# Attention scores of two image pairs in one TensorE pass, on other PSUM banks, with the transposes and tables around them recut

## The reference, cut to what matters

```python
h = tok(x)                                   # 16 x 64 x 64
tokens = concatenate([q, k, v]) = the same 64 rows three times
h = concatenate([cls_tok, h], axis=1)        # 16 x 193 x 64, class token first
attn = softmax(q k^T / 8) + rel_bias         # 8 heads of 8 features, 193 x 193
h = h + layernorm(attn @ v)                  # attention block
w = layernorm(h) @ wr + br                   # feed-forward block: router weight,
sel = top 95 of 193 tokens by w              # the largest ones take part
h = h + (mlp(sel) * w_sel scattered back) + layernorm(h)
```

## Time and profile before

| | |
|---|---|
| median of 3 runs | 88.4 us (88.22 to 92.36) |
| the profiled execution | 88.42 us, of it 86.5 us in the span |
| outside the span | 1.92 us |
| granted TensorE clock, mean | 0.985 |
| TensorE busy | 78.2 us (90%) |
| VectorE busy | 57.5 us (66%) |
| ScalarE busy | 55.8 us (65%) |
| GpSimd busy | 18.2 us (21%) |

### The profile page before, as it was taken

The page is one execution under the profiler, slowest core; times in us unless marked ns, Lnnn a source line. Parts: engine busy times, 40 slices in busy tenths (PEclk is TensorE's granted clock), DMA queues, the critical chain, the costliest instruction groups (busy, mean ns, idle before and its releaser), DMA issues.

```text
span 86.5 us, 1796 instructions
## 1 busy us (share of the span) xinstructions
PE 78.2 (90%) x638; PEld 49.8 (58%) x638; DVE 57.5 (66%) x188; ACT 55.8 (65%) x122; POOL 18.2 (21%) x31
## 2 busy tenths in 40 slices
PE   3999999999799999999998998999999799999800
PEld 1585758698478457769787865654523242446500
DVE  0299339439465994979989338389925799993860
ACT  0518247788558389885927272799999968995000
POOL 7000000000024553569150000000086300000620
PEclk9999999999999999999999999999999999999995
DMA  1937991000000000000000000000000000000045
GB/s 28 284 139 240 322 361 39 0 0 4 8 0 0 0 11 0 0 0 0 0 8 0 0 0 8 0 0 0 0 0 0 4 0 0 0 0 8 0 152 213
DMA packets 2568, 3.95 MB, mean 46 GB/s; under 512 B 544, under 2 KB 2048, under 8 KB 2560
## 3 DMA queue, kind: packets, MB, share of 16 engines
q1 hardware_dynamic: 1984, 3.31, 12.0%
q10 hardware_dynamic: 576, 0.53, 1.8%
HBM read 3.05 MB, written 0.79 MB: 44 GB/s over the span
## 4 chain that ended last, share of the span: by engine, by line
PE 78%; ACT 8%; DVE 6%; issue 3%; DVEq 1%; POOL 1%; ACTq 0%; POOLq 0%
PE bank L1398 7%; PE bank L1345 6%; PE bank L1335 6%; PE bank L1380 6%; PE bank L1207 5%; PE bank L1268 5%; PE bank L1222 4%; PE bank L1241 4%; PE bank L968 4%; PE bank L960 3%; PE bank L1444 3%; PE bank L1045 3%; PE bank L1253 2%; PE bank L1081 2%; PE bank L1063 2%
## 5 line engine op out<-in xcount | busy, mean ns | idle before, releaser
L586 ACT ACTIVATE gl<-bank,ffw 128x386 f32<-128x386 f32 x16 | 8.1, 583 | 1.0 <-PE bank L1380 1.0
L316 POOL TENSOR_TENSOR xh<-x,h 128x386 f32<-128x386 f32 x4 | 4.0, 1002 | 18.9 <-DVE x L908 18.9
L474 ACT ACTIVATE eT<-bank 128x512 f32<-128x512 f32 x8 | 4.7, 593 | 4.0 <-PE bank L1241 4.0
L1380 PE MATMUL bank<-x,ffw 64*128 64x386 f32 x32 | 6.8, 522 | 0.5 <-ACT gl L586 0.5
L284 POOL TENSOR_SCALAR xTm<-xT,xclsT 128x256 f32<-128x256 f32 x2 | 1.9, 929 | 24.0 <-DVE xT L728 24.0
L1345 PE MATMUL bank<-zq,same 128*128 128x386 f32 x16 | 6.6, 493 | 0.0
L819 DVE TENSOR_REDUCE mx<-bank 128x8 f32<-128x512 f32 x8 | 5.2, 686 | 2.1 <-PE bank L1207 2.0
L309 POOL TENSOR_TENSOR tb<-tb,cterm 128x512 f32<-128x512 f32 (+1 forms) x4 | 5.1, 1270 | 5.4 <-ACT tb L466 5.4
L1398 PE MATMUL bank<-gl,ffw 128*64 128x386 f32 x32 | 6.1, 500 | 0.0
L1241 PEld LDWEIGHTS bank<-vx,eT 128*64 128x64 f32 x128 | 4.3, 137 | 2.0 <-issue 1.2
L826 DVE TENSOR_TENSOR e_in<-bank,mx 128x512 f32<-128x512 f32 x8 | 5.2, 686 | 0.1
(11 more groups left out here) (187 smaller groups left out, 183.1 us busy)
## 6 DMA issues: line engine op xcount, KB each, us to landing
out<-zq SPq DMA_DIRECT2D x4, 193.0 KB, 2.1
toep<-toeplitz SPq DMA_DIRECT2D x1, 642.0 KB, 4.1
vx<-vx_start SPq DMA_DIRECT2D x1, 576.0 KB, 6.0
ptm<-patches_tm ACTq DMA_DIRECT2D x2, 192.0 KB, 3.4
ptm<-patches_tm SPq DMA_DIRECT2D x2, 192.0 KB, 3.5
atw<-attw SPq DMA_DIRECT2D x1, 352.0 KB, 2.8
ffw<-ffnw SPq DMA_DIRECT2D x1, 321.0 KB, 6.4
cst<-const SPq DMA_DIRECT2D x1, 131.0 KB, 4.8
```

The lines of the kernel that those rows point to most:

```text
L586: act.activation(gl[:, 2 * (m % SLOTS) + t, :], bank[UB[m % 2][t]][:, 0:GC], ACT.Gelu_apprx_tanh, bias=b1[:, m % 2:m % 2 + 1]).then_inc(s[ ...
L1380: last = pe.matmul(bank[UB[m % 2][t]][:, 0:GC], view(ffw, FFNW, "ffn_w1")[r, 128 * c:128 * c + 128], x2[r, g, :], start=True, stop=True)
```

## The change

- The eight matmuls of `scores(c)` go to eight different array tiles: pair j of the couple writes partitions 64j on, and each of the four groups of array rows (i, g) has a bank of its own, `SB = ((2, 3), (6, 7))`. VectorE reads 256 columns out of each of two neighbouring banks in one instruction.
- With rows of `e` now standing for pairs, `softmax_turn(c)` is one plain 128x128 transpose.
- Four banks are taken by scores, so `turn` has one bank (4) instead of two, but for the last half, which uses bank 7. Each turn waits for the copy of the turn before it.
- `table(t, g)` takes half of the features for all 8 pairs: two matmuls of 256 columns in place of four of 128. It now needs the values of all pairs, and every `table_turn` needs all four tables.
- `residual_rows` is split in two and moved into the token stage, on bank 7; `class_sums` is split and moved.
- The class token goes from the last to the first of the 193 columns, so that `fold_out`, the router weights and their mask are one instruction each in place of two.
- The orders of all engines are rewritten around this. In the feed-forward stage `up(6)` goes ahead of `down(3)`.

```diff
-SB, TB = (3, 4), (6, 7)
+SB, TB = ((2, 3), (6, 7)), 4
@@ fold_out
-                dve.tensor_copy(rT[:, 2 * i:2 * i + 2, 0:S - 1], src[:, :, 1:S]).then_inc(s["rT_ready"], 1)
-                dve.tensor_copy(rT[:, 2 * i:2 * i + 2, S - 1:S], src[:, :, 0:1]).then_inc(s["rT_ready"], 1)
+                dve.tensor_copy(rT[:, 2 * i:2 * i + 2, :], src).then_inc(s["rT_ready"], 1)
@@ DVE order
             fold_out(1)
+            fold_out(0)
             silu(1)
-            fold_out(0)
...
-            queries()
-            head_keys(0)
-            head_keys(1)
             dve.wait_ge(s["rsum_psum"], 1)
...
+            head_keys(0)
+            head_keys(1)
+            queries()
             values_out(0)
...
             softmax_in(2)
-            class_query_sums()
             normalise(0)
             softmax_in(3)
             normalise(1)
+            class_query_sums()
             class_query_end()
@@ router weights
-            dve.tensor_scalar(wts[:, 1:S], bank[WB][:, 0:S - 1], br_col[:, :], None, ALU.add)\
+            dve.tensor_scalar(wts[:, 0:S], bank[WB][:, 0:S], br_col[:, :], None, ALU.add)\
                 .then_inc(s["wts_ready"], 1)
-            dve.tensor_scalar(wts[:, 0:1], bank[WB][:, S - 1:S], br_col[:, :], None, ALU.add)\
-                .then_inc(s["wts_ready"], 1)
@@ PE, token stage
+            fold(1, (2,))
             project3(0)
-            fold(1, (2,))
+            class_sums(0, (2, 3))
+            residual_rows(0)
             variance4(0)
+            class_sums(0, (0, 1))
             project3(1)
-            class_sums(0)
+            residual_rows(1)
             keys(0)
-            queries(0)
+            class_sums(1, range(4))
             variance4(1)
@@ scores
-                for p in (2 * c, 2 * c + 1):
+                for j in range(2):
                     for i in range(2):
                         for g in range(2):
                             r = slice(64 * i + 32 * g, 64 * i + 32 * g + 32)
-                            last = pe.matmul(bank[SB[g]][64 * i:64 * i + 64, 256 * (p % 2):256 * (p % 2) + 256],
-                                             qT[r, p, :], k_h[r, p].rearrange("p h k -> p (h k)"),
+                            last = pe.matmul(bank[SB[g][i]][64 * j:64 * j + 64, 0:256], qT[r, 2 * c + j, :],
+                                             k_h[r, 2 * c + j].rearrange("p h k -> p (h k)"),
                                              start=True, stop=True)
@@ turn
-                if c:
-                    pe.wait_ge(s["eT_ready"], 2 * c + g - 1)
...
+                elif (c, g) == (NC - 1, 1):
+                    t = bank[SB[1][1]]
+                    pe.wait_ge(s["ein_ready"], 2 * NC)
                 else:
-                    pe.wait_ge(s["vx_ready"], 1)
-                    pe.wait_ge(s["vx2_ready"], 1)
+                    pe.wait_ge(s["eT_ready"], 2 * c + g)
@@ softmax_turn
-                for j in range(2):
-                    for i in range(2):
-                        r = slice(64 * i, 64 * i + 64)
-                        last = pe.matmul(bank[PVB[c]][r, 256 + J * j:256 + J * j + J], o[r, c, J * j:J * j + J],
-                                         ident[r, r], start=True, stop=True)
-                last.then_inc(s["pvT_psum"], 1)
+                pe.transpose(bank[PVB[c]][:, 256:384], o[:, c, :], ident).then_inc(s["pvT_psum"], 1)
@@ table
-                for b in range(4):
+                for b in range(2):
                     last = pe.matmul(out_v[:, :, :, b, :].rearrange("q a t c -> q (a t) c"),
-                                     rT[:, b, 128 * t:128 * t + rows_t],
-                                     vx[:, 4 * g:4 * g + 4, b, :, 0:D], start=True, stop=True)
+                                     rT[:, 2 * g + b, 128 * t:128 * t + rows_t],
+                                     vx[:, :, 2 * g + b, :, 0:D], start=True, stop=True)
@@ PE, attention stage
-            class_sums(1)
+            queries(0)
             values(0)
             scores(0)
-            residual_rows()
+            queries(1)
             keys(1)
             values(1)
-            queries(1)
             values_rows()
             scores(1)
...
             scores(2)
+            weigh(0, 0)
+            turn(1, 0)
             table(*TABLE[2])
-            turn(1, 0)
-            weigh(0, 0)
             weigh(0, 1)
             turn(1, 1)
             table(*TABLE[3])
             scores(3)
-            weigh(1, 0)
             softmax_turn(0)
             turn(2, 0)
+            weigh(1, 0)
+            weigh(1, 1)
             table_turn(0)
-            weigh(1, 1)
             turn(2, 1)
+            table_turn(1)
             weigh(2, 0)
-            table_turn(1)
+            softmax_turn(1)
             turn(3, 0)
+            weigh(2, 1)
+            turn(3, 1)
             table_turn(2)
-            softmax_turn(1)
-            turn(3, 1)
-            weigh(2, 1)
+            weigh(3, 0)
+            weigh(3, 1)
...
             centre("z", 0)
-            weigh(3, 0)
-            weigh(3, 1)
+            table_turn(3)
             softmax_turn(2)
             centre("z", 1)
+            softmax_turn(3)
             variance("z", 0)
-            softmax_turn(3)
-            table_turn(3)
@@ PE, feed-forward
             down(2)
+            up(6)
             down(3)
-            up(6)
             up(7)
```

## The result

The changed kernel takes **85.42 us** in the median of four runs (85.28 to 90.08), the kernel before 88.32 beside it (88.22 to 92.36): ratio 0.967 [0.9646, 0.9695]. So the changed kernel is 2.2 to 2.9 us faster, and the forecast was 2.2. The ratios compare undisturbed executions, as most kernels here, old and new, also had runs that were some two to five us longer. The profiled execution after took 85.38 us, 83.59 of it in the span (before: 88.42 and 86.54), at a mean granted clock of 0.991.

What follows compares the result with a forecast made beforehand. TensorE's own instruction list was taken to bound attention and feed-forward. Terms: 0.50 + 1.29 + 0.28 + 1.04 + 0.89 - 1.30 - 0.10 - 0.43 = 2.17; 88.4 - 2.2 = 86.2 us, 80% range 85.3 to 88.0.

Steps and rivals of the forecast that it cites:

- the likeliest case: Whole kernel: the summed forecast of 86.2 us, own range 85.6 to 87.0, chance 0.67.
- start of the chain: Attention stage: second scores start at about 32.1 instead of 32.61, with residual_rows out of the way; 0.50 us gained.
- scores in eight tiles: Attention scores: two waves of eight tiles, 0.59 instead of 1.02 a couple, three couples counting; 1.29 us gained.
- tables: Attention tables: four records of 256 columns instead of eight of 128, 0.07 saved each; 0.28 us gained.
- turn back: softmax_turn in attention: one plain transpose of 0.12 instead of eight records in 0.38, four times; 1.04 us gained.
- old waits gone: Attention stage: the three old TensorE stalls (0.26, 0.35, 0.28) vanish by reordering; 0.89 us gained.
- new waits: Single turning bank in attention: TensorE idles 0.85 before turn(1, 1) and 0.45 before turn(2, 1); 1.30 us lost.
- order at the end of attention: Fourth table turn ahead of the first variance loses 0.35, other reordering gains 0.2 and 0.05; 0.10 us lost.
- feed-forward: Feed-forward stage: two more mode changes between up and down cost 0.35, plus waiting for the gelu; 0.43 us lost.
- Rival 1: Attention scores: column tiles of one row group take turns, scores stay at 1.02; 87.9 us, chance 0.15.
- Rival 3: Turning bank in attention: TensorE idles 0.85 at each of seven turns; 90.9 us, chance 0.08.
- Rival 2: Feed-forward and turning bank: reordering costs nothing and the bank's stalls are halved; 85.2 us, chance 0.10.

Runs made afterwards that it cites:

- e5: The changed kernel run once more with no edit: times from 85.55 us, ratio 0.9745 to the kernel before.
- e7: The changed kernel with each of the four softmax_turn transposes issued three times: ratio 0.9857.
- e12: The changed kernel with each half of the residual rows multiplied twice in the token stage: ratio 0.9775.
- e2: The changed kernel with each couple's eight score matmuls issued twice into the same place: ratio 0.9889.
- e4: The changed kernel with turn(1, 1) on bank 0, so it needn't wait for the copy of turn(1, 0): ratio 0.971.
- e6: The changed kernel with turn(1, 1) on bank 0, table_out(2) ahead of weights_out(1, 0) on ScalarE, and down(3) ahead of up(6): 84.73 us, ratio 0.9601.
- e3: The changed kernel with the old feed-forward order, down(3) ahead of up(6): ratio 0.9684.
- e9: The changed kernel with residual_rows back in the attention stage as one matmul of 512 columns, second run: 88.28 us, ratio 0.986.
- e8: The changed kernel with residual_rows back in the attention stage as one matmul of 512 columns, first run: 86.83 to 94.03 us, no usable ratio.
- e10: The changed kernel without the five warming matmuls at its start, keep_busy(7, 5): ratio 0.9717.

## Why the prediction was right

The time lies in the range (85.3 to 88.0), though only 0.12 from its end, and the change is faster, as forecast; the forecast's own range for the likeliest case (85.6 to 87.0) holds e5's runs (85.55 to 86.22) but for the lowest, and not the first median. By its own steps, all from the table of points and the chains:

| term | predicted | shown |
|---|---|---|
| start of the chain | 0.50 | 0.65 (19.58 to 18.93) |
| scores in eight tiles | 1.29 | 3 x 0.40 = 1.20 |
| tables | 0.28 | 3.92 - 3.65 = 0.27 |
| turn back | 1.04 | 4 x 0.26 = 1.04 (e7 bears out the 0.12) |
| old waits gone | 0.89 | 0.89 |
| new waits | -1.30 | -(0.85 + 0.36) = -1.21 |
| order at the end of attention | -0.10 | -0.33, the rest up to 2.51, not a reading |
| norms | 0 | +0.18 |
| feed-forward | -0.43 | -0.50 |
| behind the spreading | 0 | -0.05 |
| sum | 2.17 | 2.14 |

The tables are those of the two chains between the second scores and the last turn: 1.09 + 0.87 + 1.09 + 0.87 before, 1.06 + 0.86 + 0.87 + 0.86 after. The sum is right to 0.03, by terms that are off by up to 0.23 each; that they cancel so well is luck, and so is in part the first median's place, to which a stretch adds that the sum doesn't hold (the last point below).

- **Start of the chain.** 0.15 better than forecast. The first scores come 0.13 later, not about 0.5, but the price in the token stage that was put at nothing is there: the second `xT`, behind which VectorE takes the scores, slips with them (15.54 to 15.66, counted as in the table of points). It is made good, since VectorE used to wait for the scores as well and needn't now: its first maximum starts at 16.06 in place of 16.13, the subtraction ends at 18.87 in place of 18.95, and the second scores stand 0.06 behind it in place of 0.63. The cover that the prediction saw takes no more: in e12 the second `xT` slips by as much as the first scores, and all later points with it.
- **Scores.** A wave of eight tiles costs 0.22 (e2), the 0.215 of the prediction; a couple's take 0.62 and not 0.59 since opening costs 0.19 rather than 0.16 (the eighth tile starts 0.05 behind the first, the fourth 0.02). Rival 1, that column tiles of one row group take turns, is refuted: eight records begin within 0.05 us, and e2's price is that of two waves. With it falls, for this case, what the Trainium skill says on its page "TensorE: Matmul & The Clock Gate", in "Part 3: Packing small matmuls", that a load overlaps running matmuls only when the row group differs. The trace disagrees: the two pairs share all four row groups, and the second pair's weight loads start at 31.10 while the first pair's matmuls, begun at 31.08, still run.
- **Tables.** The size is right, the reason isn't. In the same place a table saves 0.03 (1.09 to 1.06) or 0.01 (0.87 to 0.86), not 0.07; the other 0.22 is the third table's, which no longer stands right behind scores. From start to start the four together save 0.08 (3.83 to 3.75), so the 0.27 is luck.
- **The turning bank.** The places of both idles were right, and so was the first's size (0.85); the second is 0.36 and not 0.45 (by the prediction's own terms, 0.85 less the table turn's 0.35, it would have been 0.50). VectorE waits 1.09 for the fourth scores, not 2.0. The mechanism was told too narrowly, as that of a bank: e4 frees the bank and gains nothing, e6 also frees ScalarE's list and gains all of it. The prediction had the copy waiting for `weigh(0, 1)`; it hadn't said that the table's copy queues behind it and would hold TensorE as well. Rival 3 (an idle at each of seven turns) is refuted, as no other turn waits.
- **Order at the end of attention.** The -0.33 is what the other terms leave, so their errors are in it. Counted from start to start of TensorE's groups (an idle is what a group takes longer to the next start than its like elsewhere), the idles up to the first variance matmul grew from 0.94 to 1.39; this is -0.45 where the table has 0.89 - 1.21 = -0.32, and 0.13 of the rest is theirs. The fourth table turn costs 0.34, as forecast. And from the first variance matmul to the deviation it is 0.85 in place of 1.41, for the last turn back and its copy used to stand between:

```profile
53.64 0.81 PE L1345 MATMUL bank<-zq,same 128*128 128x386 f32 x2
...
54.88 0.28 ACT L485 ACTIVATE pvT<-bank 128x128 f32<-128x128 f32 x1 [0.54 <-PE bank L1253]
```

```profile
50.88 0.81 PE L1352 MATMUL bank<-zq,same 128*128 128x386 f32 x2
...
51.73 0.58 ACT L337 ACTIVATE rstd<-bank,eps 128x386 f32<-128x386 f32 x1
```

Of this 0.19 is the order's (0.96 from the start of the last turn back, which now stands in front, against 1.41, less the 0.26 counted as a turn back); 0.25 was forecast. So the order itself is worth -0.15, near the -0.10, and 0.05 has no row. The chain after leads through the last copy, but the variance matmul ends at 51.69, 0.04 ahead of the deviation, so the copy holds nothing up. Why the norms give back 0.18 was not tried.
- **Feed-forward.** The price of a change between `up` and `down` (0.20 and 0.15, from group lengths in the earlier trace rows) holds: e3 gets 0.52 back. Of the 0.49 between the groups (3.37 and an idle of 0.07, against 2.95) 0.35 is the two openings and 0.14 the wait ahead of `up(6)`, which was put at 0.08. Rival 2's first half, that this costs nothing, is refuted, and so is its second, as the idles weren't halved. That its 85.2 stands nearer to the first median than 86.2 does is due to the next point.
- **What the sum didn't hold.** The first comparison has 0.7 more than the sum. It lies ahead of the changed code, in the stretch up to the rise of the clock: 0.81 in the two profiles. In the ten profiles whose time is within 1% of their kernel's lowest, the rise lies at 8.91 and 8.86 for the two kernels of the old design and from 7.06 to 8.34 for the eight of the new. The instructions up to there are the same, and two against eight leaves open whether this is chance or whether something of the new program (where its code or its data lie, say) brings the rise forward. The two old profiles are a poor sample, too: their mean clock is 0.985 and 0.984, by a low stretch at the end of the span, and of the 32 executions of the kernel before on record with the experiments that took under 89 us only five are like that (0.982 to 0.986, 88.39 to 88.96 us); the other 27 have 0.998 or more and took 87.72 to 88.47. No trace shows where the rise lies in those. e5 has a gain of 2.25 in the times, which is that of the sum alone.

## What to carry to other kernels

Walk the written orders of all engines, with durations from rows: a sum of eight terms came out within 0.1 us of what the stages show, in part since its errors cancelled, where a share of busy time would have told nothing. When a buffer seems to hold an engine up, look at the list of the engine that frees it: what counts is the first thing in that list that waits, and a second buffer helps only if what is queued behind the wait is moved as well (e4 gained 0, with one copy moved 0.87). And compare two profiles from a point behind the rise of TensorE's clock; stages then repeat to 0.01 us, where the executions differ by 0.8.

## What the runs showed of the hardware

- **Eight tiles of 32 rows by 64 columns run at once** in float32: the 16 records of a couple take 0.62 between starts, in two waves, and two more waves cost 0.43 to 0.44 (e2). Four tiles in four waves took 1.02.
- **The place of the clock's rise varies between executions of the same code**: 7.06 and 7.76 us for two of the kernel after, and 13.11, 13.86, 19.50 and 19.92 in the profiles of e2, e9, e8 and e12, with TensorE busy without a break from 5 us on. The first variance matmul starts 0.44 us later for each us of the rise between 7.06 and 8.91 (12.15 to 12.96), and at 15.75 in the two latest. Leaving out 2 us of matmuls at the very start (e10) didn't delay it in the one profile taken (7.13).
- **The clock fell back for 6.83 us** in two profiles of a kernel that left TensorE idle for 1 us in 4 (e8, e9), and ahead of TensorE's last matmul in none of the others; in it two records of 256 columns took 1.06 in place of 0.54. The kernel before idles for 0.81 in 4 there, and the kernel after for 0.85 in the 4 from 37 to 41, without a fall.
- **The last output transfer** landed 0.5 us later in some profiles (2.69 against 2.16 from the last issue to the end, e3), the same order as the smaller terms here.
